# Expert results stored by tile position and gathered by GpSimd, instead of scattered by token

## The chip, the cores and the metric

The kernel runs on one core of one Trainium2 chip. The metric is device time in microseconds (us), lower is better; the time of the kernel before is 285.43 us, the median of 3 timed runs (284.99 to 286.11). Engines are named as the profile names them: PE (TensorE), DVE (VectorE), ACT (ScalarE), POOL (GpSimd) and SP (SyncE, which only issues transfers here).

## What is computed

A post-norm decoder layer on x of 32 x 64 tokens with 128 features, all float32: self-attention, cross-attention, and a feed-forward network with one shared expert and 15 routed ones, each followed by a layer norm. The change touches the last part only:

```python
shared_enc = _expert_stack(x, sW1, sb1, sW2, sb2).sum(0)
weights = jax.nn.softmax(x @ gW + gb, axis=-1)
topv, topi = jax.lax.top_k(weights, 3)
gated = (jax.nn.one_hot(topi, 15) * topv[..., None]).sum(axis=-2)
router_out = _expert_stack(x, rW1, rb1, rW2, rb2)
router_enc = jnp.einsum('ebtd,bte->btd', router_out, gated)
return shared_enc + router_enc + x
```

`_expert_stack` is a linear layer to 256 features (512 in the shared expert), gelu, and a linear layer back to 128. Each of the 2048 tokens needs only the three experts that it chose, 6144 rows of expert work in all.

## The kernel before

The 2048 tokens are 16 groups of 128 (a group is one row per partition); four groups are an octet, so there are four octets, c = 0 to 3. After the second layer norm a token's row (x2) goes through the router. DVE finds the three experts and, with rank counts that PE makes by matmuls (`ranks`), a slot for each of the token's three copies: a row of the DRAM tensor `x_srt`, in which each expert has its own region. The function `scatter` on POOL (L1986) then writes 48 blocks of 128 rows, one for each group and choice, by an indirect DMA with `slot` as its indices. A row is 130 words wide: the features, the gate, and the number of the row in which the result shall end. ACT makes the two further copies of the features that this needs (`payload`, L1153).

DVE next works out a table of tiles (L1757 to L1795): a tile is 128 rows of one expert, and there are NT = 62 of them at most, sorted so that the tiles whose rows come from the earliest tokens stand first. Of the 62, those past the last used one hold only padding rows.

The tile loop runs over these 62 tiles on five engines at once, each with its own program order and semaphores between them. For a tile t:
- SP loads 128 rows of `x_srt` into `x_tile` (L475, a ring of NB = 8 tiles);
- PE transposes them (L977), DVE copies the transpose out of PSUM (L1823) and copies the expert's weights into a ring (L1807, `expert_staged`);
- PE multiplies by the first weights (L985), ACT applies gelu twice (L1319), PE multiplies by the second weights (L994);
- ACT scales by the gate and copies the result to `y_tile` (L1327), into a ring of 8 that is free again when the scatter of tile t - 8 has landed;
- DVE takes the destination rows out of four tiles at a time (`tile_rows`, L1816);
- POOL scatters `y_tile` to `y_tok`, a DRAM tensor that is ordered by choice and token (L2047).

When an octet's tiles have landed in `y_tok`, SP reloads its three choices with three DMAs of 256 KB (`reload_y`, L363), DVE adds them to the octet's sum with the shared expert (L1848), makes statistics (L1854, L1858, L1861), Newton steps of the inverse root (L1875 to L1878, with a first value by ACT at L1310 for the last octet), ACT and DVE apply the norm (L1305, L1889), and SP and ACT store (L378). The octets 0 to 2 are worked on inside the loop at tiles named in `SUMS_AT` and `ROOTS_AT`, the last one after it.

The shared expert runs on PE between the other work: `shared_in` (L763), gelu on ACT (L1172), `shared_out` (L778, L783) and `shared_result` on DVE (L1603). The parts of the last octet's `shared_out` stand in the tile loop at the tiles of `SHARED_TILES`. On POOL the order is the x scatters, then the 62 y scatters, nothing else.

## Time and profile before

| | before |
|---|---|
| timed runs, median (lowest to highest) | 285.43 us (284.99 to 286.11) |
| profiled execution, span from first to last instruction | 319.6 us |
| mean granted TensorE clock in it | 0.936 |
| PE busy | 241.1 us (75%) |
| DVE busy | 221.6 us (69%) |
| ACT busy | 192.2 us (60%) |
| POOL busy | 179.0 us (56%) |
| HBM, mean over the span | 98 GB/s |

Of the profiled execution the span is its time; what lies before its first and after its last instruction has no row. It is 34.2 us above the median of the timed runs. Busy shares are averages over a program whose first half (attention) has other limits than its second: the scatters into `x_srt` run from 118.4 to 200.6 us, the tile loop from 208.9 to the end. In the timeline a row is one instruction or a run of alike ones: start, duration, engine, line, operation, and in brackets the idle time of the engine before it and what ended that.

### The profile page before, as it was taken

What the parts mean: (1) busy time and instruction counts of PE and PEld (TensorE: products, weight loads), DVE (VectorE), ACT (ScalarE), POOL (GpSimd) and SP (SyncE); (2) the same over time, 40 slices, a digit from 0 to 9 for tenths busy, and PEclk for the clock granted to TensorE, in tenths of its full rate; (3) what the DMA queues carried; (4) which work ended last, traced back from release to release, by engine and by line L of the source; (5) the groups of instructions that cost most, each with busy time, mean ns of one, the idle gap of its engine ahead of it and who ended that gap; (6) DMA issues with size and microseconds to landing.
All of it is one profiled execution on the core that took longest, in us unless ns stands there. A gap on an engine that the chain in (4) does not pass through costs nothing.

```text
span 319.6 us, 7117 instructions
## 1 busy us (share of the span) xinstructions
PE 241.1 (75%) x2283; PEld 179.8 (56%) x2283; DVE 221.6 (69%) x630; ACT 192.2 (60%) x423; POOL 179.0 (56%) x166
## 2 busy tenths in 40 slices
PE   6989989877988767996761299688868867785970
PEld 3676868655535434452451156586857757674960
DVE  6777999989999998998520497043444434856875
ACT  4697997549976976754470350344554546563665
POOL 6132755330666738985677467135656566665752
PEclk9999999999997998998978589799999999999778
DMA  7672830124000002952211133123132263354462
GB/s 218 217 213 46 181 128 2 37 67 133 2 0 2 0 4 62 378 215 49 86 58 50 44 101 108 41 61 101 53 99 76 75 187 90 91 168 123 150 185 90
DMA packets 38597, 31.89 MB, mean 100 GB/s; under 512 B 12864, under 2 KB 31552, under 8 KB 38432
## 3 DMA queue, kind: packets, MB, share of 16 engines
q1 hardware_dynamic: 34608, 23.90, 26.6%
q0 software_dynamic: 3520, 7.27, 6.7%
q8 instruction: 19, 0.31, 0.4%
q10 hardware_dynamic: 432, 0.27, 0.3%
q14 instruction: 18, 0.15, 0.2%
HBM read 19.95 MB, written 11.47 MB: 98 GB/s over the span
## 4 chain that ended last, share of the span: by engine, by line
PE 44%; DVE 27%; issue 14%; ACT 4%; another core or an unknown queue 4%; POOL 4%; DMA 1%; DVEq 0%; SPq 0%; ACTq 0%
PE psum L994 12%; PE psum L985 9%; PE psum L783 5%; DVE prob_sums L1496 4%; PE psum L763 4%; DVE maxes L1490 3%; PE psum L977 2%; PE psum L568 2%; DVE prob_sums L1410 2%; POOL x_srt L1986 2%; PE psum L585 1%; DMA xT<-x_t 1%; DVE turned_room L1421 1%; DVE maxes L1405 1%
## 5 line engine op out<-in xcount | busy, mean ns | idle before, releaser
L2047 POOL DMA_INDIRECT y_tok<-k_heads,y_rows x62 | 62.7, 1012 | 50.8 <-ACT k_heads L1327 34.4
L1319 ACT ACTIVATE k_heads<-psum,k_heads 128x128 f32<-128x128 f32 x124 | 38.7, 365 | 38.5 <-PE psum L985 33.6
L1986 POOL DMA_INDIRECT x_srt<-v_blocks,slot x48 | 48.0, 1000 | 21.3 <-issue 17.2
L994 PE MATMUL psum<-k_heads 128*128 128x128 f32 x248 | 42.4, 295 | 18.0 <-issue 12.1
L1823 DVE COPY k_heads<-psum 128x128 f32<-128x128 f32 x62 | 17.8, 289 | 48.9 <-PE psum L977 32.7
L994 PEld LDWEIGHTS psum<-k_heads 128*128 128x128 f32 x248 | 34.2, 200 | 21.9 <-issue 15.2
L985 PE MATMUL psum<-k_heads 128*128 128x128 f32 x248 | 40.6, 288 | 5.2 <-DVE k_heads L1823 4.2
L1963 POOL TENSOR_TENSOR k_heads<-k_heads,inv_sums 128x1024 f32<-128x1024 f32 x14 | 27.1, 1939 | 24.0 <-DVE inv_sums L1503 23.9
L985 PEld LDWEIGHTS psum<-k_heads 128*128 128x128 f32 x248 | 33.8, 198 | 8.5 <-DVE k_heads L1823 7.4
L1951 POOL TENSOR_TENSOR probs<-probs,inv_sums 128x512 f32<-128x512 f32 x16 | 16.8, 1050 | 28.9 <-DVE inv_sums L1415 28.7
L1327 ACT ACTIVATE k_heads<-psum,k_heads 128x128 f32<-128x128 f32 x62 | 22.9, 370 | 11.3 <-PE psum L994 9.1
L1807 DVE COPY k_heads<-expert_w 128x514 f32 x62 | 26.8, 438 | 3.6 <-issue 2.6
L686 PE MATMUL psum<-k_heads,v_pairs 128*32 128x128 f32 x256 | 17.4, 403 | 8.0 <-POOL k_heads L1963 5.1
L662 PE MATMUL psum<-q_heads,k_heads 64*64 64x256 f32 x256 | 18.9, 412 | 3.1 <-ACT k_heads L1120 1.6
L1120 ACT ACTIVATE k_heads<-psum 128x1024 f32<-128x1024 f32 x16 | 16.3, 1022 | 8.0 <-PE psum L670 8.0
L1496 DVE TENSOR_REDUCE prob_sums<-k_heads 128x64 f32<-128x1024 f32 x16 | 19.1, 1196 | 0.5 <-issue 0.5
L568 PE MATMUL psum<-k_heads,q_heads 128*128 128x128 f32 x128 | 17.5, 281 | 2.6 <-issue 0.9
L568 PEld LDWEIGHTS psum<-k_heads,q_heads 128*128 128x128 f32 x128 | 16.1, 194 | 4.9 <-issue 4.7
L1490 DVE TENSOR_REDUCE maxes<-psum 128x64 bf16<-128x1024 f32 x16 | 18.8, 1189 | 0.0
L763 PE MATMUL psum<-ctxT_k,expert_w 128*128 128x512 f32 x32 | 17.4, 688 | 0.3 <-issue 0.3
L977 PE MATMUL psum<-consts,k_heads 128*128 128x128 f32 x62 | 17.1, 278 | 0.0
L686 PEld LDWEIGHTS psum<-k_heads,v_pairs 128*32 128x32 f32 x256 | 7.7, 119 | 16.0 <-POOL k_heads L1963 7.9
(191 smaller groups left out, 530.1 us busy)
## 6 DMA issues: line engine op xcount, KB each, us to landing
expert_w<-e_w SPq DMA_DIRECT2D x1, 4369.0 KB
k_heads<-x_srt SPq DMA_DIRECT2D x62, 65.0 KB
q_heads<-y_tok SPq DMA_DIRECT2D x8, 256.0 KB
x_srt<-pad SPq DMA_DIRECT2D x16, 65.0 KB
xT<-x_t SPq DMA_DIRECT2D x4, 256.0 KB, 5.1
ctxT_k<-ctx_k SPq DMA_DIRECT2D x2, 512.0 KB, 5.5
v_scr<-v_rows SPq DMA_DIRECT2D x4, 256.0 KB, 2.8
ctxT_v<-ctx_v SPq DMA_DIRECT2D x2, 512.0 KB, 5.0
```

The lines of the kernel that those rows point to most:

```text
L568: mm = pe.matmul(bank[2 + g % 2][:, 128 * b:128 * b + 128], q_heads[:, c % 2, 4 * j + b, :], k_heads[:, c % 2, :, o:o + 32], start=(b == 0 ...
L686: mm = pe.matmul(bank[6 + p % 2][32 * q:32 * q + 32, 128 * b:128 * b + 128], v_pairs[:, p, j, :, :].rearrange("p a b -> p (a b)"), pr[:, : ...
L763: pe.matmul(shared_bank(k, a), expert_w[:, NE + h, P * a:P * a + P], x2T[:, 512 * c:512 * c + 512], start=True, stop=True).then_inc(s_shar ...
L985: mm = pe.matmul(bank[2 + t % 2][:, P * a:P * a + P], tile_weights(t)[:, P * a:P * a + P], x_tileT[:, t % 2, :], start=True, stop=True)
L994: mm = pe.matmul(bank[6 + t % 2][:, 0:E], h_tile[:, t % 2, a, :], tile_weights(t)[:, FE + E * a:FE + E * a + E], start=(a == 0), stop=(a = ...
L1319: ins = act.activation(h_tile[:, t % 2, a, :], bank[2 + t % 2][:, P * a:P * a + P], ACT.Gelu, bias=tile_weights(t)[:, EW - 2 + a:EW - 1 + a])
L1490: dve.tensor_reduce(maxes2[:, p % 2, :], psum[:, 1024 * (p % 2):1024 * (p % 2) + 1024].rearrange("p (g t x) -> p t g x", g=4, x=4), mybir. ...
L1496: dve.tensor_reduce(prob_sums2[:, p % 2, :], probs2[:, p % 3, :].rearrange("p (t h) -> p t h", t=B), AX_X, ALU.add).then_inc(s_inv_sums2, 1)
L1807: dve.tensor_copy(stage[:, t % NS, :], expert_w[:, bass.ds(expert_of[t % 4], 1), :].rearrange("p a b -> p (a b)")).then_inc(s_staged, 1)
L1963: pool.tensor_tensor(probs2[:, p % 3, :].rearrange("p (t h) -> p t h", t=B), probs2[:, p % 3, :].rearrange("p (t h) -> p t h", t=B), inv_s ...
L1986: pool.indirect_dma_start(out=x_srt, out_offset=bass.IndirectOffsetOnAxis(ap=slot[:, n:n + 1], axis=0), in_=payloads[:, g, k, :], in_offse ...
L2047: pool.indirect_dma_start(out=y_tok, out_offset=bass.IndirectOffsetOnAxis(ap=y_rows[:, t:t + 1].bitcast(mybir.dt.uint32), axis=0), in_=y_t ...
```

## The change

Three things are changed together.

Results are kept by tile position. `y_tile` is stored by SP, two tiles with one plain DMA of 128 KB, to `y_srt`, whose row 128 t + p holds row p of tile t. POOL no longer scatters results; it gathers them: 48 indirect DMAs, one for each group and choice, read 128 rows of `y_srt` into `routed_y` in SBUF. The gathers stand in POOL's order after the x scatters, in five lots: groups 0 and 1 (6 gathers, when the tiles of the first half octet are stored), groups 2 and 3 (6), and 12 for each further octet. Before a lot POOL waits for the stores, whose numbers it loads into registers from `t_landed`.

The indices of the gathers are `y_slot`. DVE makes them from `slot`: `y_mapped`, 16 operations ahead of the tile loop, makes for every octet and expert the offset between a row in `x_srt` and its place in `y_srt`, and `y_slots(c)`, 6 operations at tiles 5, 8, 18 and 26, moves an octet's slots by it. The gate is no longer carried with the row: `x_srt` is 128 words wide, `payload` and `tile_rows` are gone, ACT's copy of a result is plain, and DVE multiplies by the gate as it adds (`added`, four operations of 128 x 128 in place of one of 128 x 512).

Work is moved. Two of the eight `shared_in` go from before the tile loop into the tiles 20, 21, 23 and 24, with their gelu; `SHARED_TILES` go from (8, 14, 20, 26) to (28, 31, 34, 37). The norm of octet 0 and 1 and the sums of octet 2 stand after the loop, and the last octet's sums and statistics are made group by group.

```diff
-SUMS_AT = (39, 48, 57)
-ROOTS_AT = 52
-SHARED_TILES = (8, 14, 20, 26)
+SUMS_AT = (42, 57)
+Y_SLOTS_AT = (5, 8, 18, 26)
+SHARED_IN_TILES = (20, 21, 23, 24)
+SHARED_TILES = (28, 31, 34, 37)
...
+            def y_stored(p):
+                sp.wait_ge(s_y_tile, 2 * p + 2)
+                if p >= NY:
+                    sp.wait_ge(s_y_stored[p % NY], 16 * (p // NY))
+                sp.dma_start(y_srt[2 * P * p:2 * P * p + 2 * P, :].rearrange("(a p) e -> p a e", p=P),
+                             y_tile[:, 2 * p % NB:2 * p % NB + 2, :].bitcast(I32)).then_inc(s_y_stored[p % NY], 16)
...
             gates_turned(1)
-            shared_in(6)
-            shared_in(7)
             shared_out(2, 0)
...
                     if t >= NB:
-                        act.wait_ge(s_y_scattered[t % NB], 16 * (t // NB))
-                    act.activation(y_tile[:, t % NB, :], bank[6 + t % 2][:, 0:E], ACT.Copy,
-                                   scale=x_tile[:, t % NB, E:E + 1]).then_inc(s_y_tile, 1)
+                        act.wait_ge(s_y_stored[t // 2 % NY], 16 * (t // 2 // NY))
+                    act.copy(y_tile[:, t % NB, :], bank[6 + t % 2][:, 0:E]).then_inc(s_y_tile, 1)
...
+            def y_slots(c):
+                n = slice(12 * c, 12 * c + 12)
+                routed(dve.tensor_tensor(mapped, one_hot[:, c, :, :].unsqueeze(2).broadcast_to([P, 12, 3, NE]),
+                                         y_map[:, c, :, :].unsqueeze(1).broadcast_to([P, 12, 3, NE]), ALU.mult))
+                routed(dve.tensor_reduce(moved, mapped, AX_X, ALU.add))
...
+                dve.tensor_tensor(y_slot[:, n], slot[:, n], moved[:, :, 0], ALU.subtract).then_inc(s_y_slots, 1)
...
-                dve.tensor_tensor(acc[:, 4 * c:4 * c + 4, :], acc[:, 4 * c:4 * c + 4, :],
-                                  routed_y[k][:, 4 * c:4 * c + 4, :], ALU.add).then_inc(s_y_sum, 1)
+                for g in range(4 * c, 4 * c + 4):
+                    ins = dve.scalar_tensor_tensor(out=acc[:, g, :], in0=routed_y[k][:, g, :], scalar=gate_cols[:, g, k:k + 1],
+                                                   in1=acc[:, g, :], op0=ALU.mult, op1=ALU.add)
+                ins.then_inc(s_y_sum, 1)
...
+            def added_last(j):
+                g = 4 * (NC - 1) + j
+                dve.wait_ge(s_y_last[j], 16 * TOPK)
...
-            for t in range(NT):
-                pool.wait_ge(s_y_tile, t + 1)
-                pool.wait_ge(s_y_rows, t // 4 + 1)
-                pool.indirect_dma_start(out=y_tok, out_offset=bass.IndirectOffsetOnAxis(
-                    ap=y_rows[:, t:t + 1].bitcast(mybir.dt.uint32), axis=0),
-                    in_=y_tile[:, t % NB, :], in_offset=None).then_inc(s_y_scattered[t % NB], 16)
+            pool.wait_ge(s_landed, 1)
+            landed = [[pool.value_load(t_landed[0:1, i, k:k + 1], min_val=16 * ((max(NE, 4 * TOPK * i) + 1) // 2 // NY),
+                                       max_val=16 * (TABLE // 2 // NY)) for k in range(NY)] for i in range(NC + 1)]
+            first = (0, 2 * TOPK) + tuple(4 * TOPK * c for c in range(1, NC + 1))
+            for i in range(NC + 1):
+                c = max(i - 1, 0)
+                for k in range(NY):
+                    pool.wait_ge(s_y_stored[k], landed[i][k])
+                pool.sem_inc(s_y_through, 1)
+                pool.wait_ge(s_y_slots, c + 1)
+                for n in range(first[i], first[i + 1]):
+                    g, k = n // TOPK, n % TOPK
+                    pool.indirect_dma_start(out=routed_y[k][:, g, :].bitcast(I32), out_offset=None, in_=y_srt,
+                                            in_offset=bass.IndirectOffsetOnAxis(ap=y_slot[:, n:n + 1], axis=0)
+                                            ).then_inc(s_y_got[c] if c < NC - 1 else s_y_last[g % 4], 16)
```

The end of POOL's program before, with the semaphores that a row waits for; `v_blocks` holds the rows of x2 with their gates.

```order
L1986 DMA x_srt<-v_blocks,slot 32768x130 x3
L1974 TENSOR_TENSOR rstd<-rstd,minus_half 128x4 [waits s_ln2]
L1986 DMA x_srt<-v_blocks,slot 32768x130 x6
L1986 DMA x_srt<-v_blocks,slot 32768x130 [waits s_payloads,s_payload_gates,s_slots]
L1986 DMA x_srt<-v_blocks,slot 32768x130 x11
L1986 DMA x_srt<-v_blocks,slot 32768x130 [waits s_payloads,s_late_rows,s_payload_gates,s_slots]
L1986 DMA x_srt<-v_blocks,slot 32768x130 x11
L2047 DMA y_tok<-k_heads,y_rows 14080x128 [waits s_y_rows,s_y_tile] x62
L91 UNCONDITIONAL_BRANCH [waits s_y_scattered3,s_y_scattered4,s_y_scattered2,s_y_scattered5,s_y_scattered1,s_y_scattered6,s_y_scattered0,s_y_scattered7,s_late_rows,s_scattered]
```

The end of POOL's program after. `t_landed` are the numbers that are loaded into registers (20 such loads, of which the last two stand here), `q_heads` and `ctxT_v` hold `routed_y`.

```order
L2078 TENSOR_LOAD t_landed
L2078 ISA x2
L2078 TENSOR_LOAD t_landed
L2078 ISA x2
L2089 DMA q_heads<-y_srt,y_slot 128x128 [waits s_y_stored3,s_y_stored2,s_y_stored0,s_y_stored1,s_y_slots]
L2089 DMA q_heads<-y_srt,y_slot 128x128
L2089 DMA ctxT_v<-y_srt,y_slot 128x128
L2089 DMA q_heads<-y_srt,y_slot 128x128 x2
L2089 DMA ctxT_v<-y_srt,y_slot 128x128
L2089 DMA q_heads<-y_srt,y_slot 128x128 [waits s_y_stored3,s_y_stored2,s_y_stored0,s_y_stored1,s_y_slots]
L2089 DMA q_heads<-y_srt,y_slot 128x128
L2089 DMA ctxT_v<-y_srt,y_slot 128x128
```

The 62 scatters that each waited for one tile are gone; the gathers stand in lots of 6, 6, 12, 12 and 12, and only the first of a lot waits, for the stores of all tiles that hold its rows.

DVE ahead of the tile loop and in its first tiles, before (`k_heads<-psum` is the copy of a transposed tile, `k_heads<-expert_w` that of expert weights).

```order
L1834 TENSOR_REDUCE t_landed<-used_f 1x8
L1603 SCALAR_TENSOR_TENSOR x_rows<-v_blocks,psum 128x512
L1823 COPY k_heads<-psum 128x128 x2
L1816 TENSOR_TENSOR y_rows<-k_heads,result_rows 128x4
L1823 COPY k_heads<-psum 128x128 x2
L1603 SCALAR_TENSOR_TENSOR x_rows<-v_blocks,psum 128x512
L1807 ISA
L1807 COPY k_heads<-expert_w 128x514
L1823 COPY k_heads<-psum 128x128
L1807 ISA
L1807 COPY k_heads<-expert_w 128x514
```

The end of `y_mapped` and the first tiles, after (lines 1847 to 1850 are `y_mapped`, 1854 to 1860 are `y_slots`).

```order
L1850 TENSOR_TENSOR v_blocks<-v_blocks 128x15
L1847 TENSOR_TENSOR v_blocks<-run_data,v_blocks 128x15
L1817 COPY k_heads<-psum 128x128 x4
...
L1817 COPY k_heads<-psum 128x128
L1854 TENSOR_TENSOR v_blocks<-v_blocks 128x540
L1856 TENSOR_REDUCE v_blocks<-v_blocks 128x36
L1857 TENSOR_TENSOR v_blocks<-slot,v_blocks 128x12
L1858 TENSOR_TENSOR v_blocks<-v_blocks 128x12
L1859 TENSOR_TENSOR v_blocks<-v_blocks 128x12
L1860 TENSOR_TENSOR y_slot<-slot,v_blocks 128x12
L1809 ISA
L1809 COPY k_heads<-expert_w 128x514
```

`y_mapped` stands between the shared expert's result and the first copy of a transposed tile; the first `y_slots` stands between the copy for tile 5 and the weights for tile 7, where before there was one operation of `tile_rows` for four tiles.

PE ahead of the tile loop, before (L763 is `shared_in`, L778 and L783 are `shared_out`, L977 is the first transpose of the loop).

```order
L763 MATMUL psum<-ctxT_k,expert_w 128x512 x6
L778 MATMUL psum<-v_pairs,k_heads 128x512
L783 MATMUL psum<-expert_w,turned_room 128x128 x16
L751 MATMUL psum<-consts,probs 128x128
L763 MATMUL psum<-ctxT_k,expert_w 128x512 x4
L778 MATMUL psum<-v_pairs,k_heads 128x512
L783 MATMUL psum<-expert_w,xT 128x128 x16
L977 MATMUL psum<-consts,k_heads 128x128 x2
```

The same place after, and the tiles 20 and 21, where L982, L990 and L999 are the three steps of a tile and L770 is `shared_in_late`.

```order
L760 MATMUL psum<-ctxT_k,expert_w 128x512 x6
L785 MATMUL psum<-v_pairs,k_heads 128x512
L790 MATMUL psum<-expert_w,turned_room 128x128 x16
L748 MATMUL psum<-consts,probs 128x128
L785 MATMUL psum<-v_pairs,k_heads 128x512
L790 MATMUL psum<-expert_w,xT 128x128 x16
L982 MATMUL psum<-consts,k_heads 128x128 x2
...
L982 MATMUL psum<-consts,k_heads 128x128
L990 MATMUL psum<-k_heads 128x128 x2
L999 MATMUL psum<-k_heads 128x128 x2
L770 MATMUL psum<-ctxT_k,expert_w 128x512
L982 MATMUL psum<-consts,k_heads 128x128
```

Four of the matmuls of `shared_in`, which stood between the two last `shared_out` ahead of the loop, now stand between tiles inside it.

## Rows read from the trace of the kernel before

**Rows 1.** Page, section 5: out<-in xcount | busy, mean ns | idle before, releaser.

```profile
L2047 POOL DMA_INDIRECT y_tok<-k_heads,y_rows x62 | 62.7, 1012 | 50.8 <-ACT k_heads L1327 34.4
...
L1986 POOL DMA_INDIRECT x_srt<-v_blocks,slot x48 | 48.0, 1000 | 21.3 <-issue 17.2
```

**Rows 2.** Line 2047: duration ns min/median/max, first and last start.

```profile
L2047 POOL DMA_INDIRECT y_tok<-k_heads,y_rows x62: 953/959/1412, 212.4 to 313.2; - x62
```

**Rows 3.** Timeline of POOL: start, duration, engine, line, [idle before].

```profile
158.41 1.03 POOL L1986 DMA_INDIRECT x_srt<-v_blocks,slot  x1 [0.20 <-issue]
...
179.97 0.96 POOL L1986 DMA_INDIRECT x_srt<-v_blocks,slot  x1 [0.30 <-issue]
...
185.03 0.96 POOL L1986 DMA_INDIRECT x_srt<-v_blocks,slot  x1 [4.10 <-DVE slot L1576]
...
199.62 0.96 POOL L1986 DMA_INDIRECT x_srt<-v_blocks,slot  x1 [0.30 <-issue]
```

**Rows 4.** Waits from 160 to 205 us: total, times, longest, in us.

```profile
DVE route_in L1547 <- remote: 11.0, 1, 11.0
```

**Rows 5.** Waits from 205 to 320 us.

```profile
DVE k_heads L1823 <- PE psum L977: 32.7, 26, 6.2
```

**Rows 6.** Timeline of ACT and PE: results of tile 0 and 45, two transposes.

```profile
211.74 0.37 ACT L1327 ACTIVATE k_heads<-psum,k_heads 128x128 f32<-128x128 f32 x1 [0.31 <-PE psum L994]
...
285.95 0.27 PE L977 MATMUL psum<-consts,k_heads 128*128 128x128 f32 x1
...
286.26 0.37 ACT L1327 ACTIVATE k_heads<-psum,k_heads 128x128 f32<-128x128 f32 x1
...
286.95 0.27 PE L977 MATMUL psum<-consts,k_heads 128*128 128x128 f32 x1
```

**Rows 7.** Timeline of DVE ahead of the tile loop.

```profile
185.61 1.09 DVE L1767 TENSOR_TENSOR k_heads<-totals,row_consts 128x900 f32<-128x900 f32 x1
...
193.18 0.25 DVE L1787 TENSOR_TENSOR run_over<-run_over 128x91 f32<-128x91 f32 x1
```

**Rows 8.** Chain that ended last, from 178 to 225 us: start, us, what.

```profile
180.63 1.68 issue
...
191.91 3.57 PE psum L783 x32
...
195.59 3.44 PE psum L763 x8
...
199.02 3.69 issue
...
203.81 5.20 PE psum L783 x32
...
219.32 0.86 PE psum L778 x2
220.18 0.89 PE psum L783 x8
```

**Rows 9.** Timeline: scatter of tile 53, reload, first addition, last statistics.

```profile
300.61 0.95 POOL L2047 DMA_INDIRECT y_tok<-k_heads,y_rows  x1 [0.97 <-ACT k_heads L1327]
...
304.09 0.76 SPq L363 DMA_DIRECT2D q_heads<-y_tok  x2
...
310.59 1.49 DVE L1848 TENSOR_TENSOR x_rows<-x_rows,q_heads 128x512 f32<-128x512 f32 x2
...
314.23 0.17 DVE L1861 TENSOR_SCALAR probs<-probs 128x4 f32<-128x4 f32 x1
```

**Rows 10.** DMA view: issues, KB each, median us to landing.

```profile
xT<-x_t SPq DMA_DIRECT2D x4, 256.0 KB, 5.1
...
v_blocks<-v_scr SPq DMA_DIRECT2D x16, 64.0 KB, 2.5
...
x_rows<-x_scr SPq DMA_DIRECT2D x8, 128.0 KB, 3.0
```

**Rows 11.** Timeline of POOL: the first scatter.

```profile
118.42 1.20 POOL L1986 DMA_INDIRECT x_srt<-v_blocks,slot  x1 [1.16 <-issue]
```

More of the change, by code:

```diff
@@ L490, in _, with x_row_of @@
-            for g in range(4):
-                sp.wait_ge(s_final_v, g + 1)
-                store(sp, 0, g)
-            for k in range(NB):
-                sp.wait_ge(s_y_scattered[k], landed_all[k])
-            reload_y(sp, NC - 1)
-            for g in range(4):
-                sp.wait_ge(s_final, g + 1)
-                store(sp, 1, g)
-            for g in range(4):
-                sp.wait_ge(s_final, 5 + g)
-                store(sp, NC - 2, g)
-            for g in range(2):
-                sp.wait_ge(s_final_v, 5 + g)
+            def x_row_of(t):
+                return nc.values_load_multi_w_load_instructions(
+                    tile_of(t, 0), engines=[SP], min_val=0, max_val=NE * ROOM,
+                    skip_runtime_bounds_check_because="the table ends at the last tile's row")[1]
@@ new lines, in _ @@
+            for t in range(NB):
+                if t % 4 == 0:
+                    x_rows_at = x_row_of(t)
+                x_loaded(t, x_rows_at)
+            for t in range(NT):
+                if t + NB < NT:
+                    if t % 4 == 0:
+                        x_rows_at = x_row_of(t + NB)
+                    sp.wait_ge(s_tile_turned, t + 1)
+                    x_loaded(t + NB, x_rows_at)
+                if t % 2 == 1:
+                    y_stored(t // 2)
+            for c in range(NC - 1):
+                for g in range(4):
+                    sp.wait_ge(s_final, 4 * c + g + 1)
+                    store(sp, c, g)
@@ L504, in _ @@
+            for g in range(2):
+                sp.wait_ge(s_final_v, g + 1)
                 store(sp, NC - 1, g)
@@ L742, in ranks @@
                 if c == NC - 1:
+                    for i in range(2):
+                        pe.matmul(bk[:, 64 + NC * NE:64 + (NC + 1) * NE], ones[:, :], chosen[:, i, :], start=(i == 0), stop=(i == 1))
                     mm = pe.matmul(bk[:, 64:64 + NC * NE], ones[:, :], carry[:, 1:NC + 1, :].rearrange("p c e -> p (c e)"), start=True, stop=True)
@@ L1147, in exp_logits @@
                 act.activation(route_exp[:, :, :], route_exp[:, :, :], ACT.Exp).then_inc(s_logit_exps, 1)
-            def payload(c):
-                act.wait_ge(s_x2, 4 * c + 4)
-                for k in range(1, TOPK):
-                    act.copy(payloads[:, 4 * c:4 * c + 4, k, 0:E], x2[:, 4 * c:4 * c + 4, :]).then_inc(s_payloads, 1)
             def orT_out(c):
@@ L1920, in _ @@
                     expert_of = expert_staged(t + 2, expert_of)
+            root_seed(0, NC - 2)
+            for n in range(3):
+                root_newton(0, NC - 2)
+            sum_mean(0, NC - 2)
+            for k in range(TOPK):
+                added(NC - 2, k)
+            sum_stats(NC - 2)
             root_seed(NC - 2, NC - 1)
```

281 lines of the change are left out of this document (139 added, 142 removed).

## The prediction

> **What bounds the kernel now.** I read the grouped lines first. GpSimd issues 48 scatters into x_srt and 62 into y_tok, and each holds it for about 1.0 us [rows 1, 2], so the two groups alone are 110 of its instructions. Next its timeline: from 158.41 to 179.97 one scatter starts every 1.268 us (17 steps in 21.56 us), with 0.30 us of idle before each [rows 3]. That start-to-start time, 1.27 us, is the unit of everything below.
>
> Then the waits, since GpSimd also stands still. The span is 319.6 us, the median of the timed runs is 285.43 us: the profiled execution has 34 us that the timed runs have not. The list of waits shows where they may sit: VectorE waits 11.0 us for something the profile calls remote before the last octet's routing [rows 4], the chain has 1.68 and 3.69 us of "issue" between shared matmuls before the tile loop [rows 8], and inside the loop VectorE waits 32.7 us in 26 pieces on PE transposes [rows 5] that take 0.27 us each [rows 6]. Where nothing holds them, PE starts a tile every 1.00 us (285.95, then 286.95) [rows 6]. Nothing in the program explains the pieces, so I take them as the profiled execution's own and also work out a kernel without them.
>
> Without them GpSimd never rests. The wait of 4.10 us at 185.03 is for slots [rows 3] that come 11.0 us late [rows 4]; on time they are there before GpSimd has finished its first 18 scatters. Of 62 result tiles only 54 can hold rows: counting the routing of the reference's inputs, the tiles ready after each octet are 19, 28, 45 and 54 (15 after the first half octet); the rest are padding. So the chain is 30 x scatters and 54 y scatters back to back from 158.4: 83 steps of 1.27 us, the last starts at 263.8. It lands 2.5 us later: between the profile's 2.5 us for a 64 KB transfer [rows 10] and the 3.5 us from scatter 54's start, 300.61, to the reload behind it, 304.09 [rows 9]. The reload is three transfers of 256 KB, estimated at 4.5 us: issues and a landing of up to 5.1 us [rows 10]. From the first addition at 310.59 to the end are 9.0 us [rows 9]. The sum is 279.8 us; the 5.6 us to the median are what lies around the span and what this model misses, and I take them as equal for both kernels. PE needs about 1.0 us a tile and GpSimd 1.27: the loop is bound by GpSimd's issue.
>
> **The change part by part.** *GpSimd.* 62 scatters go, 48 gathers come. Each gather is again an indirect transfer of 128 rows of 512 bytes, so the nearest rows are the two scatters, whose means are 1000 and 1012 ns although one writes 130-word rows to x_srt and the other 128-word rows [rows 1]. I take 1.27 us a step; the bounds are 0.3 us (the time between two scatters, if generation itself were nearly free) and 1.71 us (the longest, 1.412, plus 0.30) [rows 2, 3]. What counts is where the gathers stand. An octet's gathers wait for all tiles that hold its rows. The first 24 (half octet, its rest, octet 1) need tile 28 and have run out well before tile 45. The 12 of octet 2 need the 46th tile, the 12 of octet 3 the 54th, only 8 us later, and 12 gathers take 15 us: so 24 gathers, 23 steps or 29.2 us, stand one behind another after the 46th result, where before only the remaining scatters did. GpSimd's queue holds nothing else then; the last additions wait for it. The early half octet falls in time in which GpSimd would idle, and its worth at the end is nothing. The 20 register loads of t_landed stand between the x scatters and the first gather, 12 us before that gather can start, and cost nothing.
>
> *Start of the tile loop.* The first transposes stand behind shared work on PE. Four shared_in matmuls leave that place: 3.44 us of the chain [rows 8]. VectorE gets y_mapped, 16 small operations, ahead of its first copy: one of 91 columns takes 0.25 us [rows 7], these have 15 to 45, so 0.20 us each and 3.2 us, and tiles_landed is longer by some four of them. PE's gain and VectorE's loss cancel; the bounds are -3.4 us (VectorE's part hidden under the shared results) and +0.7. The first result of the trace is copied out by 212.1 [rows 6]. Less 11.0 us [rows 4], the 1.68 and 3.69 us, and the 1.6 us by which the last shared_out (5.20 us) is longer than the one before it (3.57 us) [rows 8], that is 194, and I leave it there.
>
> *Inside the loop, to the 46th result.* 45 tiles of 1.00 us; the four shared_in matmuls that come back, 3.44 us; shared_out, moved to tiles 28 to 37 but still ahead of tile 45, 0.86 and four times 0.89, 4.4 us [rows 8]. Before, these were covered by GpSimd's slower pace; now PE is alone in front and they count. Four times y_slots stands in VectorE's queue ahead of the next expert copies: a multiply and a reduction of 540 columns, each 0.6 of the 1.09 us that a multiply of 900 takes [rows 7], and four small ones, 2.2 us in all. PE is one or two transposes ahead and hides some of it: 1.5 us each, 6 us, with bounds 0 and 8.8. The 46th result is then at 194 + 45 + 3.4 + 4.4 + 6 = 253.
>
> *The store.* SP stores two tiles with one transfer of 128 KB: an issue of 0.4 and 3.0 us to landing [rows 10], 256.4 us. GpSimd waits for that. SP's own queue alternates loads and stores; a load now stands behind a store that waits for its results, but loads run 8 tiles ahead, so nobody waits. The scaling by the gate that leaves ScalarE's copy does not shorten it.
>
> *The end.* Last gather at 256.4 + 29.2 = 285.6, landed at 288.1. The reload (4.5 us) is gone. Only one group's three additions and statistics are left behind it, about a quarter of the octet's work from 310.59 to 314.23: 1.1 us, then 5.4 us from 314.23 to the end [rows 9]: 6.5 in all. That gives 294.6.
>
> *Smaller things.* The payload copies of ScalarE go; the first scatter starts at 118.42, 1.16 us after GpSimd was free [rows 11], and no longer waits for gates: -0.5 us, between 0 and -0.9. The load of result_rows, tile_rows, half of the t_late loads and the early pad store lie beside longer work: 0.
>
> **The sum**: 294.6 - 0.5 - 279.8 = +14.3 us, so 285.4 + 14.3 = 299.7, forecast 300. Against the profiled execution itself: its 46th result is ready at 286.6 [rows 6]; with 3.4 and 6 us more in the loop, 3.4 for the store, 29.2, 2.5, 6.5 and -0.5 it would end at 337.1 against 319.6, or +17.5; if its holds hide the 9.4 us in the loop, +8.1. The two ways have the same sign, and 14.3 lies between.
>
> **Where the Trainium skill disagrees.** The trace has GpSimd held for 1.0 us by every indirect transfer, whatever it carries [rows 1]. The Trainium skill, DMA: Bandwidth & Descriptors, section "Anatomy of one DMA — SWDGE (gpsimd) path", calls descriptor generation "small, variable" and puts most of a fixed 2 us into the write's receipt at the target. By that rule queued gathers would cost almost nothing after the first, and the sum would be near 279, as the cheap end of the first rival below. The trace speaks against it for scatters; no row here shows a gather.
>
> **The rivals.** *A gather is cheap* (faster). It writes SBUF and not DRAM, and nothing in the trace is a gather. The last 12 then wait for the 54th result, 8 us and a store after the 46th: 264.4, and the end is 264.4 + 11 steps + 9.0. At 0.3 us that is 276.7, less 0.5: -3.6 us, 282. It is level with before at about 0.55 us, less than half of every scatter's step in the trace. Chance 0.08.
>
> *The loop's insertions are covered.* y_mapped and y_slots hide under shared work and PE's lead, and the 9.4 us that I charge go: 300 - 9 = 291. For it: VectorE has slack of some 0.3 us a tile. Against it: PE would be at its bound of 1.00 us and can't regain a stall. Chance 0.2 together with half covers (289 to 295).
>
> *GpSimd is slowed* (slower still). Some scatters take 1.2 to 1.41 us [rows 2]; if all gathers did, 23 steps of 1.71 are 39.3 and the time 310. Decides if the step is over 1.5. Chance 0.12. The Trainium skill, GPSIMD Engine Reference, section "1. Specifications", has GpSimd's SBUF interface shared with VectorE and contended by some of its instructions; by that the longest scatters would be those beside VectorE's work, and after the loop, where VectorE is mostly idle, the 310 would not come.
>
> *The change shows nothing* (same). Insertions covered and gathers at 1.0 us: 291 - 6 = 285. Chance 0.04.
>
> **How the numbers follow.** The forecast itself, 295 to 306, has 0.56. About 0.5% (1.4 us) is what a measurement of this kernel can tell from no change. Slower by over that: 0.56 + 0.20 + 0.12 = 0.88; within: 0.04; faster: 0.08. The range goes from 289 (covered insertions, a somewhat cheaper gather) to 311 (all gathers at the longest scatter).
>
> **What would show it.** In the profile of after: gathers as an unbroken row of 24 on GpSimd at the end, with 1.27 us a step; GpSimd idle before it on DMA stores of tiles 44 and 45, some 9 us; the tile loop on PE at 1.0 us a tile with gaps of 1 to 2 us at the four y_slots; about 6.5 us from the last landing to the end. Wrong would be a step well under 1 us, a 46th result more than 5 us away from 59 us after the first, or x scatters that no longer follow each other without a gap.

## The result and the profile after

The kernel after takes 298.93 us (median of 4 runs, 298.71 to 299.68), the kernel before 285.21 us (median of 4, 283.80 to 286.11). The ratio is 1.0493, with a 95% interval of 1.0457 to 1.0528: the change makes the kernel 13.7 us slower. The forecast was 300 us.

The profiled execution of the kernel after has a span of 297.9 us, 1.8 us less than the 299.68 us of that same execution (in the other kernels 1.7 to 2.2 us lie around the span), so nothing is held in it and it can be read against the timed runs directly. Executions that take over 1.5% longer than the fastest of their kernel are left out of the medians below, which concerns the second, the tenth and the eleventh run, and as the profiled executions of the second and the eleventh are such ones, only stretches inside one trace are read from these two.

GpSimd's timeline in the kernel after (start, duration, engine, line, operation, idle time before it and what ended that): the first and the last x scatter, the first gather of all, the first of octet 2's lot, and the last of all.

```profile
117.53 1.28 POOL L2019 DMA_INDIRECT x_srt<-v_blocks,slot  x1 [0.19 <-issue]
...
194.11 0.98 POOL L2019 DMA_INDIRECT x_srt<-v_blocks,slot  x1 [0.30 <-issue]
215.51 1.00 POOL L2089 DMA_INDIRECT q_heads<-y_srt,y_slot  x1 [20.41 <-DMA y_srt<-k_heads]
...
259.06 0.95 POOL L2089 DMA_INDIRECT q_heads<-y_srt,y_slot  x1 [8.08 <-DMA y_srt<-k_heads]
...
288.52 0.94 POOL L2089 DMA_INDIRECT ctxT_v<-y_srt,y_slot  x1 [0.30 <-issue]
```

The first x scatter comes 0.89 us earlier than in [rows 11]. The scatters that wrote results are gone, and where [rows 3] go on into them GpSimd now stands idle: 20.41 us before the first lot, 4.93 us before octet 1 (at 235.73), 8.08 us before octet 2, each time for a store into `y_srt`. From 259.06 on it never rests: 24 gathers, 23 steps in 29.46 us, 1.281 us a step. A third of the gathers (those into one of the two buffers) as a group: duration in ns as min/median/max, first and last start; under it the time to landing.

```profile
L2089 POOL DMA_INDIRECT ctxT_v<-y_srt,y_slot x16: 944/948/1245, 218.1 to 288.5; - x16
...
DMA to landing us min/median/max: 2.5/2.6/2.8
```

A gather holds GpSimd for 0.944 to 1.245 us, much as a scatter did (0.953 to 1.412 [rows 2]), and lands 2.6 us after its start.

ScalarE's copies of the first, the 46th and the 62nd result, and SP's store of the 45th and 46th:

```profile
193.54 0.27 ACT L1330 COPY k_heads<-psum 128x128 f32<-128x128 f32 x1 [0.31 <-PE psum L999]
...
255.94 0.27 ACT L1330 COPY k_heads<-psum 128x128 f32<-128x128 f32 x1
...
256.23 0.38 SPq L478 DMA_DIRECT2D y_srt<-k_heads  x1
...
273.91 0.27 ACT L1330 COPY k_heads<-psum 128x128 f32<-128x128 f32 x1 [0.65 <-PE psum L999]
```

The first result is copied out by 193.81, the 46th by 256.21; the store is issued at 256.23, and 2.83 us later the gathers start.

The end, on VectorE and then ScalarE's queue: the last group's additions, the last statistics, the last store.

```profile
291.07 0.74 DVE L1878 SCALAR_TENSOR_TENSOR x_rows<-q_heads,gate_cols,x_rows 128x128 f32<-128x128 f32 x2 [1.98 <-DMA ctxT_v<-y_srt,y_slot]
...
292.78 0.17 DVE L1886 TENSOR_SCALAR probs<-probs 128x4 f32<-128x4 f32 x1
...
294.74 1.31 ACTq L380 DMA_DIRECT2D out<-x_rows  x2
```

From the last gather's landing to the end are 6.8 us.

### The profile page after: what moved, and what is told of

The parts are those of the page before. It is cut to its first block, busy times and chain, and to the rows that moved or that the text cites. A ratio compares the mean times of both kernels' runs of the same rounds, so it can differ in the third digit from the quotient of the medians.

```text
span 297.9 us, 7043 instructions
## 1 busy us (share of the span) xinstructions
PE 232.4 (78%) x2285; PEld 175.8 (59%) x2285; DVE 236.1 (79%) x689; ACT 182.4 (61%) x419; POOL 163.7 (55%) x152
## 4 chain that ended last, share of the span: by engine, by line
DVE 41%; PE 32%; issue 11%; POOL 8%; ACT 3%; DMA 3%; DVEq 1%; SPq 0%; POOLq 0%; ACTq 0%
PE psum L990 7%; PE psum L999 6%; DVE prob_sums L1500 5%; POOL q_heads L2089 4%; DVE maxes L1494 3%; PE psum L563 2%; POOL ctxT_v L2089 2%; PE psum L790 2%; DVE prob_sums L1414 2%; PE psum L982 2%; DMA xT<-x_t 1%; POOL k_heads L1997 1%; PE psum L580 1%; DVE maxes L1409 1%; DVE expert_w L1389 1%
## 5 line engine op out<-in xcount | busy, mean ns | idle before, releaser
L1322 ACT ACTIVATE k_heads<-psum,k_heads 128x128 f32<-128x128 f32 x124 | 38.9, 366 | 40.8 <-PE psum L990 40.6
L2089 POOL DMA_INDIRECT q_heads<-y_srt,y_slot x32 | 31.1, 972 | 42.3 <-DMA y_srt<-k_heads 33.4
L990 PE MATMUL psum<-k_heads 128*128 128x128 f32 x248 | 40.2, 286 | 9.9 <-DVE k_heads L1817 9.9
L990 PEld LDWEIGHTS psum<-k_heads 128*128 128x128 f32 x248 | 33.6, 197 | 14.0 <-DVE k_heads L1817 12.8
L999 PE MATMUL psum<-k_heads 128*128 128x128 f32 x248 | 38.5, 278 | 0.3 <-ACT k_heads L1322 0.3
L999 PEld LDWEIGHTS psum<-k_heads 128*128 128x128 f32 x248 | 33.1, 194 | 0.6 <-ACT k_heads L1322 0.6
L2089 POOL DMA_INDIRECT ctxT_v<-y_srt,y_slot x16 | 16.1, 1008 | 4.9 <-issue 4.9
L982 PE MATMUL psum<-consts,k_heads 128*128 128x128 f32 x62 | 17.3, 279 | 1.0 <-DMA k_heads<-x_srt 1.0
L1330 ACT COPY k_heads<-psum 128x128 f32<-128x128 f32 x62 | 16.6, 269 | 1.0 <-PE psum L999 1.0
L681 PEld LDWEIGHTS psum<-k_heads,v_pairs 128*32 128x32 f32 x256 | 7.7, 118 | 14.3 <-POOL k_heads L1997 7.4
```

What stands on the lines that cost most here:

```text
L681: mm = pe.matmul(bank[6 + p % 2][32 * q:32 * q + 32, 128 * b:128 * b + 128], v_pairs[:, p, j, :, :].rearrange("p a b -> p (a b)"), pr[:, : ...
L982: pe.transpose(bank[t % 2][:, 0:P], x_tile[:, t % NB, :], ident).then_inc(s_tile_turned, 1)
L990: mm = pe.matmul(bank[2 + t % 2][:, P * a:P * a + P], tile_weights(t)[:, P * a:P * a + P], x_tileT[:, t % 2, :], start=True, stop=True)
L999: mm = pe.matmul(bank[6 + t % 2][:, 0:E], h_tile[:, t % 2, a, :], tile_weights(t)[:, FE + E * a:FE + E * a + E], start=(a == 0), stop=(a = ...
L1322: ins = act.activation(h_tile[:, t % 2, a, :], bank[2 + t % 2][:, P * a:P * a + P], ACT.Gelu, bias=tile_weights(t)[:, EW - 2 + a:EW - 1 + a])
L2089: pool.indirect_dma_start(out=routed_y[k][:, g, :].bitcast(I32), out_offset=None, in_=y_srt, in_offset=bass.IndirectOffsetOnAxis(ap=y_slot ...
```

## The experiments

Each run's ratio is to the kernel before on the same chip, whose median was between 284.9 and 286.1 us there. The kernel after was timed on one chip only, and executions of one kernel spread by up to 4 us on the chips of the experiments. So a time that differs from its 298.93 us by less than some 3 us shows nothing by itself; there the traces are read.

### The kernel before, profiled again

> The kernel before, unchanged, profiled again. If the held stretches of its first profile (11.0 us before the last octet's slots, 5 us before the tile loop, some 20 us in the loop) belong to that one execution, the span comes near 284 us (the kernel after has a span of 297.9 at a time of 298.9, so about 1 us lies around the span), GpSimd issues the last 30 x scatters and the y scatters in one row from about 158 at 1.27 us a step, and the 54th y scatter starts near 264. If the holds belong to the kernel, they are there again and the span is above 300; then the sum of the prediction rested on a wrong picture of before.

No line is changed. Measured: 285.12 us. From the view of the cores (span and mean granted TensorE clock):

```profile
core 0: 283.3 us, clock 0.955
```

GpSimd's timeline in it: the first of the last 30 x scatters, the only gap of over 0.6 us, the scatter of tile 53. Then ScalarE's copies of the 46th and the 62nd result and VectorE's first addition for the last octet:

```profile
157.92 1.03 POOL L1986 DMA_INDIRECT x_srt<-v_blocks,slot  x1 [0.20 <-issue]
...
206.36 0.95 POOL L2047 DMA_INDIRECT y_tok<-k_heads,y_rows  x1 [1.02 <-ACT k_heads L1327]
...
265.70 1.25 POOL L2047 DMA_INDIRECT y_tok<-k_heads,y_rows  x1 [0.30 <-issue]
```

```profile
253.31 0.37 ACT L1327 ACTIVATE k_heads<-psum,k_heads 128x128 f32<-128x128 f32 x1
...
274.50 0.37 ACT L1327 ACTIVATE k_heads<-psum,k_heads 128x128 f32<-128x128 f32 x1 [0.53 <-PE psum L994]
274.57 1.49 DVE L1848 TENSOR_TENSOR x_rows<-x_rows,q_heads 128x512 f32<-128x512 f32 x2
```

The holds were those of one execution. GpSimd issues without a rest from 157.92, as the prediction took it, but for one gap of 1.02 us, and tile 53 starts at 265.70 (the prediction: 263.8). What was not seen: the first addition does not wait for the reload. The last octet's reload is issued at 268.57, and VectorE, busy with octet 2's root behind its loop, reaches the addition at 274.57 without having waited.

Nor does GpSimd's issue set the loop's pace, though it has hardly any rest. The waits of ScalarE's result copy from 192 to 275 us, and PE's waits for loads of `x_tile` from 192 to 266 us (total, times, longest, in us):

```profile
ACT k_heads L1327 <- PE psum L994: 1.3, 4, 0.5
```

```profile
PE psum L977 <- DMA k_heads<-x_srt: 6.0, 4, 2.6
```

ScalarE waits for PE alone, never for a place in the ring that a scatter has to free. GpSimd follows each of the 62 results by 0.3 to 4.9 us, by 1.7 us at the 46th and by 0.9 at the 54th. The copies of the results run from 192.82 to 253.31 for the first 46, 1.34 us a tile, at the loop's own pace. As far as the waits show, scatters act on it only through landings that SP waits for. PE's wait of 2.20 us at 200.00 ends with a load that stands behind the last x scatter, and that of 2.56 us at 237.89 with one that stands in SP's order behind octet 0's reload (issued at 232.12, when its scatters had landed).

### Late work of the shared expert moved behind the 46th result

> The kernel after, with the late shared-expert work of the last octet moved from tiles 20 to 37 to tiles 47 to 59 (two tables of numbers). In the profile of after it adds about 3.5 + 0.7 us (first layer) and 4.4 us (second layer) between the first and the 46th result. Queue theory (the end is the 46th result, its store, then 24 gathers one behind another on GpSimd): the 46th result comes 8 to 8.6 us earlier and the time falls by as much, to 290.5 +- 1. Rival (the start of the last two lots is set by something other than PE's pace, a store's landing or VectorE's sums): no change, 298.9, or less than 3 us.

```diff
-        SHARED_IN_TILES = (20, 21, 23, 24)
-        SHARED_TILES = (28, 31, 34, 37)
+        SHARED_IN_TILES = (47, 48, 50, 51)
+        SHARED_TILES = (53, 55, 57, 59)
```

Measured: 294.87 us, ratio to before 1.0339 (1.0238 to 1.0441), and in the eleventh run, the same kernel again, 293.19 us and 1.0301 (1.0195 to 1.0407). It gains some 4 to 6 us, not 8. Its 46th and 62nd result on ScalarE, its last gather on GpSimd, and all that VectorE waits for from 262 us to the end (total, times, longest, in us):

```profile
250.04 0.27 ACT L1330 COPY k_heads<-psum 128x128 f32<-128x128 f32 x1
...
276.40 0.27 ACT L1330 COPY k_heads<-psum 128x128 f32<-128x128 f32 x1 [0.65 <-PE psum L999]
```

```profile
282.62 0.95 POOL L2089 DMA_INDIRECT ctxT_v<-y_srt,y_slot  x1 [0.31 <-issue]
```

```profile
DVE k_heads L1817 <- PE psum L982: 5.3, 4, 3.7
DVE probs L1911 <- ACT probs L1313: 0.3, 1, 0.3
```

From the first result (194.47) to the 46th are 55.6 us where the kernel after needs 62.4: the queue did come forward. But from the last gather's start to the end are 13.3 us where they were 9.4, and behind the loop VectorE waits for no gather at all: only 0.3 us for ScalarE's root. It works from the 62nd result to the end. So the queue theory is not enough: there is a second chain, VectorE's own program behind the loop, which in the kernel after ends little earlier than the queue.

### Index work in single steps

> The kernel after, with the index work on VectorE cut into single steps, one or two operations a tile, from tile 1 on (the last octet's from tile 54 on), in place of 16 operations ahead of the loop and four blocks of six. Queue theory: the loop starts 2.4 us earlier (transposes are ready at 187.2 to 187.8, the first copy comes at 189.95 in after) and of the four stalls of 1.4 to 1.8 us (6.1 us in all) some 1.8 us stay for the two long operations of each of three octets: -6.6 us, 292.3 +- 1. Rival (PE was not stopped by VectorE, the gaps at those tiles are its own): less than 2 us gained.

```diff
-        Y_SLOTS_AT = (5, 8, 18, 26)
+        Y_INDEX_AT = (*range(1, 26), *range(54, 60))
...
-            y_mapped()
             for t in range(NT):
...
-                if t in Y_SLOTS_AT:
-                    y_slots(Y_SLOTS_AT.index(t))
+                if t in Y_INDEX_AT:
+                    next(y_index)
```

(each `next` makes two or three operations of `y_mapped`, or one of `y_slots`.) Measured: 294.77 us, ratio 1.0333 (1.0252 to 1.0413), 4.2 us below the kernel after; 6.6 was expected. The first result, a step of `y_slots` between two results, and the 46th result; then the first late gather and the last:

```profile
189.16 0.27 ACT L1330 COPY k_heads<-psum 128x128 f32<-128x128 f32 x1 [0.42 <-PE psum L999]
...
202.80 0.27 ACT L1330 COPY k_heads<-psum 128x128 f32<-128x128 f32 x1
...
203.11 0.16 DVE L1870 TENSOR_TENSOR y_slot<-slot,v_blocks 128x12 uint32<-128x12 uint32 x1
...
203.81 0.27 ACT L1330 COPY k_heads<-psum 128x128 f32<-128x128 f32 x1
...
249.95 0.27 ACT L1330 COPY k_heads<-psum 128x128 f32<-128x128 f32 x1
```

```profile
253.75 0.99 POOL L2106 DMA_INDIRECT q_heads<-y_srt,y_slot  x1 [8.06 <-issue]
...
284.12 1.07 POOL L2106 DMA_INDIRECT ctxT_v<-y_srt,y_slot  x1 [0.30 <-issue]
```

The loop starts 4.4 us earlier, at 189.16 against 193.54, but the first result lies anywhere between 190.6 and 194.5 in the traces of the kernels that keep the block ahead of the loop, and at 190.11 in the fifth run, which has lost the block too. From the first to the 46th result are 60.8 us, 1.6 less than in the kernel after, where 4.3 less were expected. Single operations did not stop PE: at tiles 11 to 13 and 16 to 18, which have one each, results come 1.00 to 1.01 us apart. The long operations of the three blocks that are left cost 1.4, 1.1 and 0 us, near the 1.8 expected. The rest of the gain went into the tiles 1, 2 and 6, which come 0.9, 0.5 and 0.8 us late beside two or three operations of `y_mapped` each. Tiles 1 and 2 come as late in five kernels that keep the block ahead, so only the 0.8 us can be laid to this edit; what causes the others is not settled.

The 46th result is 6.0 us earlier in this trace and the last gather 4.40: the lot starts 3.5 us after the store's issue at 250.24 instead of 2.8, and its 23 steps take 30.4 us instead of 29.5. VectorE still waits for gathers from 262 us on:

```profile
DVE x_rows L1896 <- DMA ctxT_v<-y_srt,y_slot: 2.7, 2, 1.9
DVE x_rows L1888 <- DMA ctxT_v<-y_srt,y_slot: 1.9, 1, 1.9
```

That is 4.6 us, so here the queue is still in front, and the second chain has no part in what was missed.

### Eight of the late gathers left out

> The kernel after, where the second and third choice of octet 2 are not gathered (8 of the 24 late gathers left out; the sums of that octet read what stands in the buffer). Queue theory: the lot of octet 3 then starts when tile 53 is stored, at 267.1 in place of 274.75 in the trace of after, 7.6 us earlier: 291.3 +- 0.7. If a gather's price were its landing and not its issue, or the end were set by VectorE's work after the loop, nothing changes: 298.9.

```diff
-                    dve.wait_ge(s_y_got[c], 16 * 4 * TOPK)
+                    dve.wait_ge(s_y_got[c], 16 * 4 * (1 if c == NC - 2 else TOPK))
...
+                    if c == NC - 2 and k > 0:
+                        continue
```

Measured: 296.83 us, ratio 1.0422 (1.0340 to 1.0504): 2.1 us below the kernel after, where 7.6 was expected. In the traces the end is 4.8 us earlier (293.1 against 297.9 us), but the one is the fastest of four executions and the other the slowest. The first late gather and the last one, and VectorE's waits from 262 us on:

```profile
259.39 0.94 POOL L2091 DMA_INDIRECT q_heads<-y_srt,y_slot  x1 [8.08 <-DMA y_srt<-k_heads]
...
282.10 1.05 POOL L2091 DMA_INDIRECT ctxT_v<-y_srt,y_slot  x1 [0.30 <-issue]
```

```profile
DVE k_heads L1817 <- PE psum L982: 1.1, 3, 0.4
DVE probs L1911 <- ACT probs L1313: 0.3, 1, 0.3
```

Octet 3's lot starts at 267.44, as expected, and the last gather 6.4 us earlier. VectorE no longer waits for any, and goes from its loop to the end without a wait for one. In the kernel after it does wait, in the same stretch:

```profile
DVE x_rows L1878 <- DMA ctxT_v<-y_srt,y_slot: 2.5, 2, 2.0
DVE x_rows L1870 <- DMA ctxT_v<-y_srt,y_slot: 1.9, 1, 1.9
```

That is 4.4 us in all: by so much the queue ends behind the second chain. With VectorE's program as it is, a shorter queue can give no more than about that.

### Three moves together

> The kernel after with three moves at once: the index work in single steps from tile 1 on, the late shared-expert work behind the 54th result (its first layer at tiles 54 to 58, its second at 60 to 63, its sum after the loop), and octet 0's sums from tile 42 to tile 48. From the two traces before: first result 189.2, 46th 239.0, and GpSimd's lot of octet 1 ends at 242.6. Queue theory alone: 24 gathers from 242.7, last at 272.2, 9.4 us behind it: span 281.6, time 283.4, faster than the kernel before. Two chains (the queue, and VectorE's own program after the loop, which in the last two runs took 19 us from the 62nd result to the end without a wait): the 62nd result comes near 267.5, the span ends near 286.7, the time is 288.5, slower than before.

```diff
-        SUMS_AT = (42, 57)
+        SUMS_AT = (48, 57)
...
-        SHARED_IN_TILES = (20, 21, 23, 24)
-        SHARED_TILES = (28, 31, 34, 37)
+        SHARED_IN_TILES = (54, 55, 57, 58)
+        SHARED_TILES = (60, 61, 62, 63)
...
-                if t == SHARED_TILES[-1] + 2:
-                    shared_result(NC - 1)
...
+            shared_result(NC - 1)
             dve.wait_ge(s_acc, NC)
```

with the single steps of the third run. Measured: 286.96 us, ratio to before 1.000 (0.9964 to 1.0037): all of the loss is back, and nothing more. All 48 gathers and all of the index work are still there. Its first and last gather, and VectorE's waits:

```profile
212.70 1.00 POOL L2105 DMA_INDIRECT q_heads<-y_srt,y_slot  x1 [16.89 <-DMA y_srt<-k_heads]
...
274.59 0.95 POOL L2105 DMA_INDIRECT ctxT_v<-y_srt,y_slot  x1 [0.30 <-issue]
```

```profile
DVE k_heads L1817 <- PE psum L982: 1.9, 1, 1.9
DVE probs L1929 <- ACT probs L1313: 0.3, 1, 0.3
```

The 48 gathers are now one unbroken row from the first lot's store on: 47 steps in 61.9 us, 1.317 us each, most of them beside the loop. With 9.4 us behind it this queue alone would end at 284.0; VectorE, which waited for no gather, ended the span at 285.3. The two chains end within 1.3 us of each other, and the two-chain sum (288.5) was nearer than the queue alone (283.4), with an error of 1.5.

### Without the early half octet

> The kernel after without the early half octet: all 12 gathers of octet 0 stand in one lot that waits for the 19 tiles of octet 0. Both theories: GpSimd then gathers octet 0 from about 224 to 239, octet 1 to about 255, and is free before the store at 259 that the 24 late gathers wait for: no change, 298.9 +- 0.5. A rival in which the early half takes work out of the end would show at least +3 us.

```diff
-            first = (0, 2 * TOPK) + tuple(4 * TOPK * c for c in range(1, NC + 1))
+            first = (0, 0) + tuple(4 * TOPK * c for c in range(1, NC + 1))
```

Measured: 298.73 us (the kernel after: 298.93), ratio 1.0394 (1.0343 to 1.0445). Neither the time nor the ratio shows the 3 us or more of the rival. The first gather of octet 2:

```profile
260.02 1.17 POOL L2089 DMA_INDIRECT q_heads<-y_srt,y_slot  x1 [7.06 <-issue]
```

Octet 0 starts at 221.98, 6.5 us later, and GpSimd still stands idle for 7.06 us before octet 2's lot, the one that counts, which starts at 260: the early half buys time in which GpSimd is idle.

### Gathers of half the rows

> The kernel after, where the gathers of octets 2 and 3 take only the first 64 of the 128 rows (the other half of those octets is left out). It prices a gather: if GpSimd's time goes by rows, an instruction of 0.95 us becomes about 0.48 and a step 0.78; if it is a price for each transfer, the step stays 1.25. By rows the last gather comes at about 277 in place of 288.5 and VectorE's own chain, near 293, sets the span; by transfers the span stays at 297.9.

```diff
-                    pool.indirect_dma_start(out=routed_y[k][:, g, :].bitcast(I32), out_offset=None, in_=y_srt,
-                                            in_offset=bass.IndirectOffsetOnAxis(ap=y_slot[:, n:n + 1], axis=0)
+                    pool.indirect_dma_start(out=routed_y[k][0:P if c < NC - 2 else P // 2, g, :].bitcast(I32), out_offset=None, in_=y_srt,
+                                            in_offset=bass.IndirectOffsetOnAxis(ap=y_slot[0:P if c < NC - 2 else P // 2, n:n + 1], axis=0)
```

Measured: 299.53 us in one run. The first and the last of the 24 gathers of 64 rows:

```profile
259.66 0.90 POOL L2089 DMA_INDIRECT q_heads<-y_srt,y_slot  x1 [8.29 <-DMA y_srt<-k_heads]
...
288.59 0.91 POOL L2089 DMA_INDIRECT ctxT_v<-y_srt,y_slot  x1 [0.30 <-issue]
```

23 steps take 28.93 us, 1.258 us each, against 1.281 with 128 rows. After the loop an instruction takes 0.90 us in place of 0.94. Between 64 and 128 rows the price is nearly all by the transfer, not by the row, and half the data saves 0.5 us of the queue.

### One store for each tile

> The kernel after with one store for each tile (62 of 64 KB) in place of one for two tiles (31 of 128 KB). Both theories: the store of the 46th result starts at the same time and lands about as late; SP has 31 more issues of 0.4 us in a loop in which it waits for results: no change, 298.9 +- 0.5. Rival (SP is near its limit with two loads of 0.55 us and table loads for two tiles): the loop gets slower and the time rises by 2 us or more.

```diff
-                if t % 2 == 1:
-                    y_stored(t // 2)
+                y_stored(t)
```

(with `y_stored` moving one tile, and counts of 32 in place of 16 where they wait). Measured: 299.57 us (297.76 to 301.45), ratio 1.0536 (1.0430 to 1.0642): no difference from the kernel after that these runs could show. What storing in pairs costs or gives is not shown beyond that.

### Less work for VectorE behind the loop, in two kernels

> The kernel after without the 18 Newton operations that VectorE does behind the loop for octets 0 to 2 (their roots keep the first value, so the scale of those rows is a little off). VectorE then has 3.6 us less to do behind the loop. Two chains, the queue of gathers in front: VectorE waits for the last gathers in the kernel after, so nothing changes, 298.9 +- 0.5. If VectorE's own program behind the loop were the bound: 295.3.

> The kernel with the late shared-expert work behind tile 46 (as in the second run), again without those 18 Newton operations. Two chains: there VectorE worked without a wait from the loop to the end while the last gather had come 5.9 us earlier; 3.6 us less for VectorE gives a time 3 to 3.6 us below that of the same kernel with them (queue: last gather at 282.6 and 9.4 us behind it, 292.0). If something else held that kernel back, no change.

> The kernel of the second run again, beside the two light ones: about 295.8, 3 us below the kernel after and 3 to 3.6 us above its light version.

```diff
-            for n in range(3):
-                root_newton(0, NC - 2)
...
-            for n in range(3):
-                root_newton(NC - 2, NC - 1)
```

Measured: the kernel after without these 18 operations 300.92 us (299.88 to 302.58), so no gain. The kernel of the second run without them 291.33 us (290.12 to 291.87), with them 293.19 us (292.82 to 293.75) beside it: 1.9 us, less than the 3 to 3.6 expected, but the two ranges do not touch. VectorE's waits in the light version of the kernel after, then in that of the late kernel:

```profile
DVE x_rows L1878 <- DMA ctxT_v<-y_srt,y_slot: 4.5, 3, 2.1
DVE x_rows L1870 <- DMA ctxT_v<-y_srt,y_slot: 3.7, 1, 3.7
```

```profile
DVE k_heads L1817 <- PE psum L982: 1.7, 3, 1.2
DVE probs L1911 <- ACT probs L1313: 0.3, 1, 0.3
```

In the first VectorE turns the 3.6 us into waiting: 8.2 us for gathers where it was 4.4. In the second it waits for no gather, as in the second run, and the kernel ends earlier. The same edit tells which chain is in front.

## Why the prediction was right

**The bound before** was wrong, and that its sum came out near is luck. The prediction says that the loop is bound by GpSimd's issue and that the last additions stand behind the last scatter and the reload. The second profile shows GpSimd's row without a rest, as was read out of a trace in which it rested for 34 us, but a row that follows the results by 0.3 to 4.9 us and whose issue sets no pace: the loop's own 1.34 us a tile happens to lie near GpSimd's 1.27, and the first addition waits for no reload. The terms then sum to 279.8 against a span of 283.3: the scatter of tile 53 came 1.9 us later, and the first addition 8.9 us behind its start, where 2.5 + 4.5 = 7.0 was put. The sum for after was 294.1 against 297.9. Both were low by nearly the same, 3.5 and 3.8 us, so that the difference of 14.3 stood (measured 13.7); that the two misses cancel was taken, not known. Of the 5.6 us that the prediction puts around the span, 1.8 us lie there.

**The price of a gather.** Taken 1.27 from the scatters, measured 1.281. The rival with a cheap gather falls. The half-row gathers fit with a price that carries over from scatters: it hardly depends on how much is moved. Of the 2.6 us from a gather's start to its landing only the last gather's stand at the end of the queue, while 0.94 us of issue and 0.30 of gap are paid for each. The Trainium skill, DMA: Bandwidth & Descriptors, section "Anatomy of one DMA — SWDGE (gpsimd) path", holds descriptor generation to be small against a receipt of most of 2 us; the price by that rule, almost nothing after the first gather, did not come.

The slowed GpSimd, with 1.71 us a step, falls as well: in the kernel after the longest gather beside the loop took 1.245 us, and those after it all 0.94 to 0.95. The Trainium skill, GPSIMD Engine Reference, section "1. Specifications", has GpSimd's SBUF interface shared with VectorE and contended by VectorE's instructions with two SBUF inputs, among others. The trace does not bear that out as the reason for the longer gathers: after the loop VectorE is not idle, as the prediction had it, but busy for 11.4 of the 13.4 us from 276.0 to 289.4, at first with additions of two such inputs, and the gathers beside it stay at 0.94 to 0.95. What lengthens those beside the loop stays open.

**The queue of 24.** It started at 259.06 (forecast 256.4), its last gather at 288.52 (285.6). Store to gather took 2.83 us (3.4), landing 2.55 (2.5), the rest 6.8 (6.5).

**The 46th result** came 62.4 us after the first instead of 59. The four y_slots are as forecast. The first of them in ScalarE's and VectorE's timeline, with PE's first matmul behind it:

```profile
196.04 0.71 DVE L1854 TENSOR_TENSOR v_blocks<-v_blocks 128x540 f32<-128x540 f32 x1
...
197.80 0.27 ACT L1330 COPY k_heads<-psum 128x128 f32<-128x128 f32 x1
...
198.97 0.71 PE L990 MATMUL psum<-k_heads 128*128 128x128 f32 x4 [1.17 <-DVE k_heads L1817]
...
200.24 0.27 ACT L1330 COPY k_heads<-psum 128x128 f32<-128x128 f32 x1
```

Results come 2.44 us apart here, one of 1.00 us and a stall of 1.44; the four stalls sum to 6.1 us (forecast 6.0). The term that was missing: octet 0's sums, now at tiles 42 to 45 and four operations each. The chain that ended last runs through VectorE there (start, us, what):

```profile
249.48 1.05 DVE x_rows L1870 x4
```

Tile 45 comes 6.4 us behind tile 41 instead of 4, so 2.4 us. The four `shared_in` cost 4.2 us (forecast 3.4) and `shared_out` 4.4, as forecast. That these would count only now, because GpSimd's slower pace covered them before, was wrong: before, the same stretch took 60.5 us at the loop's own pace, with parts of `shared_out` visible in it at 0.9 us each, and with the 6.0 us of waits for loads, which are gone from it after. So the loop lost 1.9 us in all, not 9.4.

**The start of the loop** was set at no change, and it held: 193.81 against 194. y_mapped took 3.0 us (forecast 3.2). Its end was on the path, for PE's first product waits behind it:

```profile
190.29 1.21 PE L990 MATMUL psum<-k_heads 128*128 128x128 f32 x4 [2.21 <-DVE k_heads L1817]
```

**Smaller things.** The first x scatter comes 0.58 us earlier than in the second profile of before (118.11), as forecast (0.5). Against the prediction ScalarE's copy of a result did get shorter without the gate, 0.27 us where it was 0.37. Two of its rivals are reckoned wrongly: a gather would have to cost about 0.63 us, not 0.55, for the two kernels to come out level (264.4 + 11 x 0.63 + 9.0 - 0.5 = 279.8), and the 9.4 us of the covered insertions are `shared_in` and `y_slots`, without `y_mapped`.

**What the prediction did not see** is how near the second chain is. Where the two kernels part, in us from the start of the span (results by the start of ScalarE's copy):

| | before, second profile | after |
|---|---|---|
| first result | 192.82 | 193.54 |
| 46th result | 253.31 | 255.94 |
| 62nd result | 274.50 | 273.91 |
| end | 283.3 | 297.9 |

Up to the last result the kernels differ by at most 2.6 us, and at the last result by 0.6. All that the change costs stands behind it: 8.8 us before, 24.0 after, of which VectorE waits 4.4 for gathers; most of the rest is its own work. The prediction forecast a GpSimd that VectorE waits for at the end, which is so, but by 4.4 us only. The rest is that octet 2's sums and the roots of octets 0 and 1, which the kernel before made inside the loop, moved behind it, and that octet 2's sums need gathers that end behind the last result. How much each part of this work costs was not measured, but for the 18 Newton operations.

The experiments that expected a shorter or earlier queue to pay in full missed by this: 4 to 6 us instead of 8 in the second run, 2.1 instead of 7.6 in the fourth. The third (4.2 instead of 6.6) missed for reasons of its own, since VectorE waits for the queue there. Only with both chains moved forward, in the fifth run, did the loss come back.

## What to carry to other kernels

In this kernel an indirect transfer costs its issuing engine a step of about 1.25 us, with 64 rows or 128, so count transfers, and count above all those that can only start after the last producer: the last of 54 scatters that followed the producer one by one started 0.9 us after the result it moved (tile 53), the last of 24 late gathers 24.3 us after that result (288.52 against 264.23). An engine without a rest need not be the bound: ask whether anything waits for it. Before you shorten a queue, look at what the consumer waits for behind it: 4.4 us of waiting was all that a shorter queue alone could win, and the next bound stood there. A span far above the timed runs is a reason to profile again before summing.

## What had not been expected of the hardware

Halving the rows of a gather, and so its bytes and indices, shortened GpSimd's instruction only from 0.94 to 0.90 us. And the profiled execution of the same program was 319.6 us once and 283.3 us the next time, with a clock of 0.936 and 0.955; what held the first is not settled.
